# Attention and mixture-of-experts layer: the fourth group's preparation moved, the shared second weight's high halves converted by transfers

## What is computed

```
x = x + attention(layernorm(x), ctx, ctx, lengths)        # 8 heads of 32 channels, keys = values = ctx, scale by log(length)
h = layernorm(x)
top 2 of 8 experts per row (softmax of h @ gate_w), capacity 320 rows per expert and rank
expert e:  y = gelu(h @ w1[e] + b1[e]) @ w2[e] + b2[e] + gelu(h @ wd[e]) @ wu[e]
shared:    s = gelu(h @ sw1 + sb1) @ sw2 + sb2 + gelu(h @ swd) @ swu
x = x + sum over the row's experts of weight * y  +  0.2 * s
```

## Time and profile before

| | us |
|---|---|
| median of 3 runs | 1390.07 |
| lowest, highest | 1388.09, 1390.71 |
| profiled execution, own time | 1389.32 |
| its span | 1387.5 |
| PE busy | 1337.6 |
| DVE busy | 816.6 |
| ACT busy | 687.6 |
| POOL busy | 253.4 |

### The profile page before, as it was taken

How to read it: one execution, slowest core, us unless ns; L and a number is a source line. 1 busy time by engine, 2 the same in 40 slices (tenths; PEclk the granted TensorE clock), 3 DMA queues, 4 the chain that set the end, 5 groups by cost and what they waited for, 6 DMA issues and landing times.

```text
span 1387.5 us, 27045 instructions
## 1 busy us (share of the span) xinstructions
PE 1337.6 (96%) x11151; PEld 965.9 (70%) x11213; DVE 816.6 (59%) x1337; ACT 687.6 (50%) x1024; POOL 253.4 (18%) x219
## 2 busy tenths in 40 slices
PE   5788999999999999999999999999999999999997
PEld 2252737464655546485888889998888888888895
DVE  7786778686887877763734626446264362552620
ACT  4776666667575766663423425334253342442421
POOL 4720010010010141423202104022030030300202
PEclk9899999999999999999999999999999999999999
DMA  9613131313132232408545567555564565544402
GB/s 271 210 47 92 51 95 39 107 47 107 47 82 65 69 70 92 123 17 196 162 116 154 128 131 191 122 159 130 131 168 124 133 176 129 153 117 104 99 2 39
DMA packets 136747, 155.89 MB, mean 112 GB/s; under 512 B 59065, under 2 KB 79689, under 8 KB 136626
## 3 DMA queue, kind: packets, MB, share of 16 engines
q1 hardware_dynamic: 124338, 128.97, 32.1%
q0 software_dynamic: 12288, 25.21, 10.0%
HBM read 109.47 MB, written 34.15 MB: 104 GB/s over the span
## 4 chain that ended last, share of the span: by engine, by line
PE 83%; DVE 6%; ACT 6%; issue 3%; DMA 0%; another core or an unknown queue 0%; POOLq 0%; POOL 0%; ACTq 0%; DVEq 0%
PE banks L1776 25%; PE banks L1806 24%; PE banks L1692 9%; PE banks L1710 8%; PE banks L1632 4%; PE banks L1580 3%; PE banks L1612 3%; DVE rowmax L1244 2%; ACT hidden L1033 2%; ACT QS L1020 2%; DVE late_stage L1265 1%; PE banks L1828 1%; PE banks L1641 1%; ACT hf L1079 1%; PE banks L1666 1%
## 5 line engine op out<-in xcount | busy, mean ns | idle before, releaser
L1806 PE MATMUL banks<-hidden,w2h 128*128 128x0 bf16 x2048 | 313.0, 273 | 0.0
L1033 ACT ACTIVATE hidden<-banks,scales 128x512 f32<-128x512 f32 x256 | 170.3, 686 | 105.4 <-PE banks L1612 68.2
L1806 PEld LDWEIGHTS banks<-hidden,w2h 128*128 128x128 bf16 x2048 | 198.5, 98 | 25.6
L1806 PE MATMUL banks<-hidden,w2l 128*128 128x0 bf16 x1024 | 195.6, 273 | 0.0
L1244 DVE TENSOR_REDUCE rowmax<-banks 128x1 f32<-128x512 f32 x256 | 172.9, 685 | 32.5 <-PE banks L1580 30.9
L1395 DVE TENSOR_TENSOR w1l<-stage,w1h 128x2048 bf16<-128x2048 f32 x32 | 73.2, 2292 | 199.5 <-ACT w1h L1110 199.5
L1127 ACT ACTIVATE hf<-banks,b1cols 128x640 f32<-128x640 f32 x128 | 101.7, 795 | 178.5 <-PE banks L1776 173.1
L1710 PE MATMUL banks<-w2h,hidden 128*128 128x512 bf16 x498 | 179.0, 379 | 1.1 <-issue 1.0
L1134 ACT ACTIVATE yT<-banks 128x640 f32<-128x640 f32 (+1 forms) x32 | 22.1, 691 | 270.1 <-PE banks L1806 270.1
L1776 PE MATMUL banks<-eth,w1h 128*128 128x0 bf16 x1024 | 136.0, 276 | 0.0
L1776 PE MATMUL banks<-etl,w1h 128*128 128x0 bf16 x1024 | 135.9, 276 | 0.0
(11 more groups left out here) (192 smaller groups left out, 1972.7 us busy)
## 6 DMA issues: line engine op xcount, KB each, us to landing
stage<-in_L_ffn_w SPq DMA_DIRECT2D x64, 1024.0 KB
split_parts<-hidden SPq DMA_DIRECT2D x16, 512.0 KB, 5.7
QS<-split_parts SPq DMA_DIRECT2D x48, 128.0 KB, 2.6
KS<-split_parts SPq DMA_DIRECT2D x48, 128.0 KB, 3.3
xin<-in_x SPq DMA_DIRECT2D x16, 256.0 KB, 3.5
cin<-in_ctx SPq DMA_DIRECT2D x16, 256.0 KB, 3.5
out_rows<-xin SPq DMA_DIRECT2D x16, 256.0 KB, 2.0
normed_rows<-x2r SPq DMA_DIRECT2D x16, 256.0 KB, 3.5
```

Source lines behind the costliest of these rows:

```text
L1033: ac.activation(prob[n % NPH], bank(score_bank[unit]), ACT.Exp, scale=scales[:, g // 2:g // 2 + 1]).then_inc(s_exp, 1)
L1806: issued = mm(half_of(bank(b0 + j)).shape_from_register(bank_cols(e, j)), w[:, fb, rows], half_of(a[:, fb, :], j).shape_from_register(slot ...
```

## The change

- `prepare(3)` is no longer in `side` of k = 0. It is stepped twice in each step of k = 1 of the first window, ahead of `side` there: statistics in n = 16, rstd in 17, norm and the ACT pair in 19, `x_lo` in 20, `c_lo` and `bounce` in 21. In n = 19 its norm stands before den(0), and in n = 20 and 21 `x_lo` and `c_lo` stand between den(0), attn(0) and resid(0).
- ACT splits only quarters 2 and 3 (steps 4 and 8). The high halves of sw2 (n = 4 to 7) come by four transfers that POOL issues at steps 12, 13, 14 and 15, from the fp32 weight in DRAM to the bf16 `w2h` (512 rows of 2 KB read each). The fp32 loads to `hstage` stay, for the low halves.
- The low pieces of sw2 are put in the list at steps 20, 22, 24 and 28, four each; in steps 20 and 21 a second one may go. They wait for their transfer instead of ACT. The last three fall in the up pass.
- `fills(1)` stands at n = 1 instead of n = 29 and waits for the pieces before it in the list.
- PE's first down product no longer waits for eight ACT splits; it still waits for all 32 low pieces.

```diff
@@ exponentials_and_down
-                    side += [prepare(g + 3)] if w else [prepare(g + 2), prepare(g + 3)]
+                    side.append(prepare(g + 3 if w else g + 2))
...
                 if w == 0:
-                    if k * UNITS + i in QUARTERS:
-                        split_quarter(2 + QUARTERS.index(k * UNITS + i))
+                    n = k * UNITS + i
+                    if n in QUARTERS:
+                        split_quarter(2 + QUARTERS.index(n))
                     else:
                         low_piece()
+                    if n in CASTS:
+                        add("w_cast", 4 + CASTS.index(n))
+                    if n in CAST_LOWS:
+                        pieces.extend((4 + CAST_LOWS.index(n), a) for a in range(4))
+                    if n in (CAST_LOWS[0], CAST_LOWS[0] + 1):
+                        low_piece()
...
-                    if k == 1 and i == UNITS - 3:
+                    if k == 0 and i == 1:
                         add("fills", 1)
...
+                if w == 0 and k == 1:
+                    one_of(fourth, 2)
                 if i >= (ONES if k else 5 if w else 0):
                     one_of(side, 1 if k == 0 and w and i < LATE else 2)
@@ work_order
-    pieces, left_over = [], []
-    QUARTERS = (4, 8, 13, 18, 23, 28)
+    pieces, left_over, fourth = [], [], [prepare(3)]
+    QUARTERS, CASTS, CAST_LOWS = (4, 8), (12, 13, 14, 15), (20, 22, 24, 28)
@@ pool_program
-                        pool.wait_ge(s_wlog, 28)
+                        pool.wait_ge(s_wlog, lows_by_fills)
...
+                elif kind == "w_cast":
+                    n = unit[1]
+                    pool.wait_ge(s_wlog, 4 if n < 6 else 8)
+                    gp.dma_start(w2h[:, (n - 4) * 4:(n - 4) * 4 + 4, :],
+                                 sw2.rearrange("(k p) d -> p k d", p=P)[:, (n - 4) * 4:(n - 4) * 4 + 4, :]).then_inc(s_cast[n - 4], 16)
                 elif kind == "w_lo":
...
-                    pool.wait_ge(s_whi, n + 1)
-                    if n >= 4:
+                    if n < 4:
+                        pool.wait_ge(s_whi, n + 1)
+                    else:
+                        pool.wait_ge(s_cast[n - 4], 16)
+                        pool.wait_ge(s_hstage[n], 16)
                         pool.wait_ge(s_wlog, 12 if n < 6 else 16)
@@ pe_program, first down product
-                            pe.wait_ge(s_whi, 8)
                             pe.wait_ge(s_wlog, 32)
```

More of the change, by code:

```diff
@@ L616, in build @@
         s_whi, s_wlo, s_wlog = sem("s_whi"), sem("s_wlo"), sem("s_wlog")
+        s_cast = [sem(f"s_cast{i}") for i in range(4)]
         s_wd, s_wdc, s_wu, s_wuc, s_rankb = (sem(n) for n in ("s_wd", "s_wdc", "s_wu", "s_wuc", "s_rankb"))
@@ L678, in build @@
         exps_by = {unit: sum(u[0] == "exp" for u in plan[:n]) for n, unit in enumerate(plan) if unit[0] == "scatter"}
+        lows_by_fills = sum(unit[0] == "w_lo" for unit in plan[:plan.index(("fills", 1))])
         def place_bank(part):
@@ L710, in split_no @@
         def split_no(j):
-            return 8 + j + 1
+            return 4 + j + 1
         def sync_program(sp):
@@ L1053, in act_program @@
                     q = n % 4
-                    dst = w1h[:, :, q * 512:q * 512 + 512] if n < 4 else w2h[:, q * 4:q * 4 + 4, :]
+                    dst = w1h[:, :, q * 512:q * 512 + 512]
                     act.wait_ge(s_hstage[n], 16)
-                    if n in (4, 6):
-                        act.wait_ge(s_wlog, 4 if n == 4 else 8)
                     ac.activation(dst, hstage[n].rearrange("p (a w) -> p a w", w=512), ACT.Copy).then_inc(s_whi, 1)
```

## The result

The changed kernel takes 1393.00 us (median of ten runs, 1391.36 to 1393.66), the one before 1389.29 (ten runs, 1388.09 to 1390.71): ratio 1.0021 [1.0013, 1.0030], so a little slower (1.8 to 4.2 us by that interval). Its profiled execution took 1393.26 us with a span of 1391.4. The forecast was 1389.0 and 1.0 us of gain; the time lies inside the range, the sign is wrong.

A forecast was written before the change was run, and what follows sets the result against it. No single engine was taken to bound the two phases, with PE nearly full behind them. Terms -2.2 + 2.0 - 0.8 = -1.0 us gave 1388.3 for the profiled execution, 1389.0 as median forecast; range 1383.3 to 1394.3.

The forecast's parts named there:

- rival 3: Issuing the converting transfers holds POOL at 3.7 us each, making norm(3) late: +5.6 us, 1395.7; chance 0.13.
- MS of group 1 ready: End of group 0's phase: without group 3's preparation on ACT and DVE, MS comes 2.2 us earlier, at 45.1.
- MS ready to end of values(0,3): From MS through the next two values products on PE: no gain counted from a faster clock, 0.
- values(0,3) to turn(0): Group 1's phase: moved preparation delays norm2(0) on DVE, so PE's turn(0) starts at 67.1, 2.0 us lost.
- turn(0) to rank: End of group 1's phase: without ACT's last split the shared rank starts at 74.75, 0.8 us gained.
- Phase A: Group 0's time, 28.4 to about 52 us: loses group 3's preparation, so MS comes 2.2 us earlier.
- Phase B, the DVE chain: Group 1's time, 52 to 75.5 us: 1.2 us wait for ACT plus two 0.8 us subtractions before norm2(0); 2.0 lost.
- Splits 5 and 6: ACT's splits in group 1's phase: removal worth nothing, behind PE's slow product and DVE's later norm2 respectively.
- split 7: ACT's split at 70.27 us, ahead of the first L1678: removal gains 0.8 us, not 1.9.
- rival 1: PE's clock stays up and the two slow values products run faster: -3.6 us, 1386.5; chance 0.22.
- Rival 2: ACT's splits bound group 1's phase and the DVE chain is hidden: -7.6 us, 1382.5; chance 0.13.
- Rival 4: Transfers delay group 2's stack loads to 62.6 us, score(2,0) wanting them at 59: +1.0 us, 1391; chance 0.09.

The follow-up runs named there:

- after_again: The changed kernel, unchanged, profiled a second time; 1392.13 us in one run.
- prep_only: The kernel before with only prepare(3) moved to the second group's phase, ACT's splits and fills as before; 1388.07 us against 1388.05, ratio 1.0002.
- after_ms_wait: The changed kernel with POOL's first converting transfer waiting until MS of group 1 is written; 1389.13 us against 1389.34 for the kernel before, ratio 0.9995.
- casts_only: The changed kernel with prepare(3) back in its old place, converting transfers and early fills kept; 1386.14 us, 0.9988 of the kernel before.
- after_spaced: The changed kernel with POOL's wait for MS, x_lo(3) moved to DVE's wait for rstd2(0), c_lo(3) behind norm2(0); 1386.17 us against 1390.61 before, ratio 0.9970.
- prep_late: The changed kernel with prepare(3) stepped only from step 9 of the second group's phase, behind norm2(0); 1391.07 us, 1.0023 of the kernel before.
- casts_ms_wait: The changed kernel with prepare(3) in its old place and POOL's first converting transfer waiting for MS; 1388.73 us, 0.9999 of the kernel before.
- spaced_warm: after_spaced plus matmuls nobody reads, put where PE idled; 1385.76 us against 1390.61 for the kernel before, ratio 0.9960.
- before_warm: The kernel before plus matmuls nobody reads, put where PE idled; 1387.46 us against 1390.61 for the kernel before, ratio 0.9981.

## Why the prediction was wrong

The forecast was a gain of 1.0 us and the kernel lost. The time still lies in the range, which is luck: the range reached up to 1394.3 to take in half of rival 3, and rival 3 did not happen.

The sum by its own terms, against after_again, which like the profile of before has the fast first product:

| step | forecast | measured |
|---|---|---|
| MS of group 1 ready | -2.2 | 46.81 - 47.26 = -0.45 |
| MS ready to end of values(0,3) | 0 | 10.69 - 10.55 = +0.14 |
| values(0,3) to turn(0) | +2.0 | 8.64 - 7.33 = +1.31 |
| turn(0) to rank | -0.8 | 10.69 - 10.37 = +0.32 |
| sum | -1.0 | +1.32 |

**Phase A is the step that failed first.** Up to the last row maximum the working holds: MS could start at 43.60 instead of 45.68, 2.1 us early. But the two MS instructions then took 3.2 us instead of 1.5. The prediction asked of POOL only when it would be done, and wrote "hidden"; it did not ask what stood on POOL at the instant of MS. Before, MS was held too: it was ready at 47.26, 0.08 behind the end of POOL's five subtractions (40.48 + 6.70 = 47.18). In every profile here, an MS instruction of group 1 that meets a subtraction ends 0.05 to 0.1 us behind one's end, and a second one that meets none takes 0.23. So what counts is when POOL's next subtraction ends. After the move alone that was at 45.47 (prep_only: MS ready 45.56, -1.7). In the changed kernel the first transfer's issue, 1.02 us, stands ahead of that subtraction and puts its end at 46.71 (after_again: 45.54 + 1.17), and MS was ready at 46.81. After_ms_wait shows it from the other side: 2.16 to 0.23 us once both stand behind MS. What no run shows is why the second instruction, which began at 44.64 during the issue, did not slip in before the subtraction recorded at 45.54.

The prediction took from the page that bears on this only the half that did not happen. The Trainium skill, "SBUF — State Buffer", section "SBUF: two separate sides", says that GpSimd and a VectorE instruction of certain kinds (in a two-port mode, or with two SBUF inputs against a GpSimd instruction that reads SBUF) share one pair of ports as a lock that the first to start holds for its whole instruction, the other waiting. The trace agrees on VectorE's waiting (its end 0.05 to 0.1 us behind the subtraction's, each time). The blocked descriptors do not show: an issue took 1.02 us in the changed kernel and 1.02 in after_ms_wait, and the casts of wdh, which the prediction feared for it, took 0.48 us beside the next issues (48.19 us in the changed kernel), where they took 3.47 beside subtractions before. Of the other rule weighed, that many descriptors cost little more (the Trainium skill, "DMA: Bandwidth & Descriptors", section "Anatomy of one DMA — SWDGE (gpsimd) path"), the trace agrees: 1.02 us for 512 rows, 2.34 for the next three, where the earlier trace rows has 0.93 for 128.

**Phase B, the DVE chain: mechanism right, size too large by 0.7.** The wait of `x_lo(3)` for ACT was 1.10 us (forecast 1.2), each subtraction held up what follows by 0.6 us (61.22 to 61.83 and 63.17 to 63.77; forecast 0.8), and the turn starts right behind norm2. That is 2.3 us where the prediction has 2.8, and of these the splits had hidden 0.8 (casts_only; it says 0.9); the 0.2 left of the 0.7 is not explained. after_spaced got 2.5 us of this stretch back by taking the wait and one subtraction out. Splits 5 and 6 are worth nothing only because the moved preparation makes DVE the last: where it stays, casts_only's turn came 0.7 to 0.8 us sooner without them.

**Phase B, split 7: sign wrong.** The 0.8 us were counted as if values(1,1) kept its 2.62 us. It took 3.64 or 3.65 in all four executions. PE had waited 1.80 and 0.82 us ahead of the turn in the changed kernel, against 0.19 and about 1.0 in casts_only and prep_late, where the product took 1.92. (The waits near the turn are not the whole reason: casts_ms_wait has 0.19 and 1.06 too, and took 3.45.) With 1.0 more, -0.8 becomes about +0.2, and +0.3 was measured. prep_only has the same 3.63. In casts_only the gain was 1.9 us. The prediction had this in one clause of rival 1 ("so the product behind it may be slower") and gave it no price.

**The rivals.** Rival 1: values(0,2) stayed slow (3.54) in the changed kernel; it was half true in prep_only (values(0,3) 1.92, values(0,2) 2.94), and it lost to the same clock later (values(1,1) 3.63). Rival 2: casts_only has the splits gone and the preparation unmoved, and gained 1.9 us, not 5.4, so the chain of waits had named a shared end. Rival 3: the four issues took 3.4 us of POOL together (1.02 and then 0.76 to 0.85 each, forecast 1.5 each) and were hidden, though a reader of the changed kernel's chain of waits could think otherwise (start, us, what):
```profile
48.22 2.26 POOL w2h L924 x3
50.48 2.43 issue
...
58.16 7.48 issue
```
The two "issue" pieces, 9.9 us, are gaps for which the chain found no releaser: it had strayed onto an engine with time to spare. DVE waited only 0.68 us for rstd(3) and then 4 us for PE. Rival 4 happened in part: group 2's six loads, which had landed by 53.68 us, landed 60.73 us at the latest in the changed kernel and 61.41 in after_again (the rival has 62.6). In its three executions with a fast first product the first score of group 2 starts 0.04 or 0.05 us behind the last load, in after_again with 0.40 us of PE idle for it. DVE's chain set the turn all the same, so it cost little; in spaced_warm it was the bound. The 512-row transfers landed in 10.9 us (median), the first 0.9 us before its use.

**What stays open.** Like for like the steps give 1.7 to 1.8 us at 90 us, of which the second window gives 0.6 to 0.7 back (0.56 in prep_only, so this comes with the moved preparation; granted clock from 116 to 132 us 0.89 in the changed kernel, 0.79 before). That leaves 1.1 us. The mean spans of the four profiles differ by 1.75 us (1389.25 less 1387.5), the medians of the ten runs by 3.7, and the ratio allows 1.8 to 4.2. Single chips and executions differ by as much as the rest: the first product's level is worth 1.4 us, the stretch near 620 us 1.5. That stretch was slow in two of four executions after, in none of four before, and also in after_ms_wait, casts_ms_wait and spaced_warm; whether the changed kernel is given to it, and why the first product's level varies, no run settles.

## What to carry to other kernels

When a step is moved so that a short critical instruction runs at another time, look up what the neighbour engine does at that very moment, not only whether the neighbour is done in time: one 16-column instruction of VectorE, held until GpSimd's subtraction ended, went from 1.1 to 2.2 us and was ready 1.25 us later than with the move alone. When PE is made to wait, price the product behind the wait at its slow duration as well; and when it waits anyway, matmuls without a use may be a cheap gain (before_warm 0.9981 of the time), but put them where the product behind is the last of the chain, and not where they can hold up work that is ready. When transfers are added, look at when the loads beside them land (2.6 us became 7.7 here): a load that still comes in time can be the next bound. Before a microsecond is explained from two profiles, take a second profile of each kernel.

## What the runs showed of the hardware

- A VectorE instruction of 128x16 elements took 0.23 us with POOL waiting or issuing transfers, and up to 1.11 when it met a POOL subtraction; it took 2.16 or 2.17 when it began during an issue with a subtraction behind it. A cast of 9x512 in after_ms_wait, begun in the same way at 47.54, took 2.19 (0.65 in the changed kernel).
- A converting transfer of 512 rows of 2 KB costs POOL 0.8 to 1.0 us to issue. With four of them under way, six loads of 128 KB on the hardware queue took 7.7 us (median) to land instead of 2.6.
- Two traces of one kernel can differ by 44 matmul records and 7 us of PE's busy time (before: 11151 and 11195 records).
- The granted clock in the windows can stand at 1.00 while matmuls run at the lower level. In the window 28.4 to 47.3 of the changed kernel it is 1.00, and yet in its PE timeline a matmul of 512 columns takes 0.61 us there (0.38 in others) and the first product's half 1.94 (1.04):
```profile
34.81 0.61 PE L1600 MATMUL banks<-KS,QS 96*128 96x512 bf16 x1 [0.94 <-ACT hidden L1056]
```
